# Decoder layer on one core: the first half-group of the self-attention in two blocks of 256 queries

## The reference

```python
q = x @ W_q
latent_kv = (k + v) @ W_down_kv
k_rec = (latent_kv @ W_up_k)...                 # 16 heads of 8 dimensions
v_rec = (latent_kv @ W_up_v)...
scores = einsum('bhqd,bhkd->bhqk', qh, k_rec) / sqrt(d)
decay = exp(-0.01 * abs(t[:, None] - t[None, :]))
attn = softmax(scores * decay, axis=-1)         # all 1024 keys for each of 1024 queries
out = einsum('bhqk,bhkd->bhqd', attn, v_rec) ... @ W_o
# then: logits = (x' @ W.T + b) @ ctx.T + mask, softmax, @ ctx; then the feed-forward net
```

## Time and profile before

| | |
|---|---|
| time, median of 3 runs | 554.35 us (554.33 to 556.05) |
| the profiled execution | 554.33 us, span 552.6 us |
| TensorE busy | 499.6 us (90%) |
| VectorE busy | 362.4 us (66%) |
| ACT busy | 336.2 us (61%) |
| GpSimd busy | 171.1 us (31%) |
| chain that ended last | PE 72%, DVE 20%, issue 3%, DMA 2%, ACT 2% |
| mean granted TensorE clock | 0.963 of 2.4 GHz |

### The profile page before, as it was taken

One profiled execution on the slowest core, in us unless ns is written; L12 is line 12 of the kernel. 1 busy time (PEld: TensorE's weight loads), 2 busy tenths in 40 slices (PEclk: granted clock), 3 DMA queues, 4 the chain that ended last, 5 costly groups with the idle time before them and its releaser, 6 DMA issues.

```text
span 552.6 us, 9809 instructions
## 1 busy us (share of the span) xinstructions
PE 499.6 (90%) x3494; PEld 327.1 (59%) x3494; DVE 362.4 (66%) x874; ACT 336.2 (61%) x659; POOL 171.1 (31%) x292
## 2 busy tenths in 40 slices
PE   8359999999999999989979979989797997989997
PEld 7206333333333333324549979879797997878886
DVE  6889988888788878704454466646666465654344
ACT  4627778787778777876664826537373562737420
POOL 6810125444444453235442221321222122210000
PEclk9758999999999999999999989989999998999999
DMA  8985400051007000031696423333342333300000
GB/s 243 284 256 121 88 2 2 4 134 41 1 3 166 10 2 2 1 117 39 165 325 187 124 76 116 93 114 92 83 121 79 116 91 115 114 16 6 1 6 7
DMA packets 27957, 49.23 MB, mean 89 GB/s; under 512 B 4140, under 2 KB 15860, under 8 KB 27332
## 3 DMA queue, kind: packets, MB, share of 16 engines
q1 hardware_dynamic: 27156, 47.87, 31.3%
q0 software_dynamic: 224, 0.54, 0.4%
q10 hardware_dynamic: 528, 0.18, 0.2%
HBM read 43.67 MB, written 4.72 MB: 88 GB/s over the span
## 4 chain that ended last, share of the span: by engine, by line
PE 72%; DVE 20%; issue 3%; DMA 2%; ACT 2%; POOL 1%; SPq 0%; DVEq 0%; ACTq 0%; POOLq 0%
PE banks L975 48%; PE banks L1084 11%; PE banks L1240 6%; DVE banks L802 6%; PE banks L1095 2%; DVE logits L878 2%; DVE fa L914 1%; PE banks L980 1%; DMA operands<-query_parts 1%; DVE qc_lo L849 1%; DVE xn L923 1%; DVE fa L913 1%; DVE fa L909 1%; ACT probs L669 1%; DVE f_small L905 1%
## 5 line engine op out<-in xcount | busy, mean ns | idle before, releaser
L669 ACT ACTIVATE probs<-banks 128x512 f32<-128x512 f32 x288 | 160.2, 599 | 49.1 <-PE banks L975 43.5
L802 DVE CUSTOM_DVE_ANT_0 banks<-banks,decay 128x1024 f32<-128x1024 f32 x128 | 155.0, 1244 | 31.4 <-PE banks L975 30.8
L975 PE MATMUL banks<-operands 112*128 112x512 bf16 (+4 forms) x736 | 148.0, 332 | 21.2 <-DMA operands<-query_parts 14.2
L975 PEld LDWEIGHTS banks<-operands 115*128 115x128 bf16 (+1 forms) x736 | 55.2, 98 | 126.9 <-ACT probs L669 55.1
L975 PEld LDWEIGHTS banks<-mem,pT 128*128 128x128 f32 (+1 forms) x816 | 108.5, 196 | 7.9
L975 PE MATMUL banks<-mem,pT 128*128 128x128 f32 (+1 forms) x816 | 112.1, 280 | 0.0
L690 ACT ACTIVATE pT<-banks 128x512 f32<-128x512 f32 (+1 forms) x104 | 60.4, 581 | 53.7 <-PE banks L1240 53.7
L878 DVE CUSTOM_DVE_ANT_0 logits<-banks,mring 128x512 f32<-128x512 f32 (+1 forms) x85 | 56.2, 667 | 43.2 <-PE banks L975 22.0
L532 POOL TENSOR_SCALAR_AFFINE_SELECT probs<-probs 128x128 f32<-128x128 f32 x128 | 37.3, 294 | 108.8 <-ACT probs L669 106.9
L1084 PE MATMUL banks<-probs,v_ext 128*32 128x512 f32 x512 | 68.2, 605 | 0.1
L975 PE MATMUL banks<-memT_hi,qc_hi 128*128 128x512 f32 (+1 forms) x104 | 51.0, 491 | 18.7 <-DVE cmax L878 18.7
(11 more groups left out here) (170 smaller groups left out, 515.4 us busy)
## 6 DMA issues: line engine op xcount, KB each, us to landing
mring<-in_mask_BxSxS_ik SPq DMA_DIRECT2D x39, 512.0 KB, 3.5
operands<-key_parts SPq DMA_DIRECT2D x24, 192.0 KB
operands<-query_parts SPq DMA_DIRECT2D x21, 192.0 KB
key_parts<-operand_parts SPq DMA_DIRECT2D x10, 256.0 KB, 3.3
mem<-in_ctx SPq DMA_DIRECT2D x3, 832.0 KB, 8.9
mask<-in_mask_BxSxS_ik SPq DMA_DIRECT2D x9, 256.0 KB, 2.9
pT<-in_mask_BxSxS_ik SPq DMA_DIRECT2D x9, 256.0 KB, 3.0
query_parts<-operand_parts SPq DMA_DIRECT2D x4, 384.0 KB, 5.3
```

The source lines that it names most:

```text
L669: act.activation(probs[:, to, :], PS[:, u % 3, :], ACT.Exp).then_inc(s_p, 1)
L802: dve.tensor_tensor_reduce(out=rows, in0=rows, in1=decay[:, off:off + S], scale=1.0, scalar=-3.0e38, op0=ALU.mult, op1=ALU.max, accum_out= ...
L975: return pe.matmul(o, a, b, start=start, stop=stop, skip_group_check=alone)
```

## The change

The first half-group is done in two blocks of 256 queries. Its units go tile by tile instead of head by head, so that after 8 units the maxima of the first 256 queries are there for all four heads. `BOUNDS` is 8, 16, 32, 48, ... 128; there are nine sets of shift rows. Set 0 (8 rows) goes out with six DMAs of SP and six of ACT, set 1 with twelve of SP, the others with six as before. Pairs 0 and 1 are the first block, pairs 2 and 3 the second: a score unit is then one key tile for two heads. The loop starts after 15 turns (`FIRST_TURNS`), and pairs 0 to 7 have five turns each, so that from pair 8 on the turns stand as before (15 + 40 = 23 + 32).

`parts_sb` moves into the second operand buffer, which frees ACT's first copy of the memory from its wait; instead GpSimd waits for the written parts before it sets that buffer's spare rows. TensorE turns three chunks of memory ahead of the first unit and one chunk in each of the next ten turns. SP's order becomes: group 0 in, `load_shift(0)`, group 1's lower operands, `load_shift(1)`, group 1's upper operands, `load_shift(2)`, `load_shift(3)`. The weight scales move to units 46, 64 and 80, the quantization to pairs 7 to 27.

```diff
+    FIRST_TURNS = 15
+    FULL_LEAD_PAIR = 8
+    HALF_PAIRS = 4
+    HQ = BANK // 2
+    BOUNDS = [UNITS // 2] + [UNITS * (g + 1) for g in range(NG * NH)]
+    MEM_FIRST = 3
     MEM_FRONT = 19
-    SCALE_UNITS = (28, 36, 44)
-    QUANT_PAIR = 3
-    MEM_UNIT = 8
+    SCALE_UNITS = (46, 64, 80)
+    QUANT_PAIR = 7
...
-            parts_sb = sb0("operand_parts", [P, 4, PARTS, S], BF16)
...
+        parts_sb = ops[1][:, :, :, :].rearrange("p w h n -> p (w h n)")[:, 0:4 * PARTS * S].rearrange(
+            "p (w i n) -> p w i n", w=4, i=PARTS)
...
+        def turns_of(n):
+            if n < FULL_LEAD_PAIR:
+                return FIRST_TURNS + 5 * n, 5
+            return UNITS + MAX_LEAD + 4 * n, 4
...
+        def half_keys(n):
+            qb = n // 2
+            off = [kt for kt in range(NT) if kt // 2 != qb][n % 2 * 3:n % 2 * 3 + 3]
+            return [off[0], 2 * qb + n % 2] + off[1:]
...
+        def load_half_shift(eng, i, w):
+            for part in range(PARTS):
+                for t in range(2):
+                    q0 = i * HQ + t * P
+                    eng.dma_start(queries(0, w, 0)[SHIFT_ROW + part:SHIFT_ROW + part + 1, :, q0:q0 + P],
+                                  shift_parts[t * HG:(t + 1) * HG, part, :]).then_inc(s_sh[i], 16)
...
-            def load_shift(hg):
+            def load_shift(i):
+                hg = max(i - 1, 0)
                 g, half = hg // NH, hg % NH
-                sp.wait_ge(s_sp, hg + 1)
+                sp.wait_ge(s_sp, i + 1)
                 for w in (QL, QU):
...
+                    if i == 0 and w == QL:
+                        load_half_shift(sp, 0, QL)
+                    if i == 1:
+                        load_half_shift(sp, 1, w)
...
             load_operand(0, QU)
             load_operand(0, KU)
+            load_shift(0)
             load_operand(1, KL)
             load_operand(1, QL)
-            load_shift(0)
+            load_shift(1)
             load_operand(1, QU)
             load_operand(1, KU)
-            load_shift(1)
             load_shift(2)
+            load_shift(3)
...
             pool.wait_ge(s_iota2, 1)
+            pool.wait_ge(s_scr0, 16)
+            for w in range(4):
+                pool.wait_ge(s_scr[w], 16 * (SLOTS if w in (KL, KU) else 1 if w == QL else NH))
...
-                if c == 0:
-                    act.wait_ge(s_scr0, 16)
...
                 if step >= MEM_LAG:
                     mem_low(step - MEM_LAG)
+            act.wait_ge(s_sp, 1)
+            load_half_shift(act, 0, QU)
...
+                if i >= 1:
+                    dve.wait_ge(s_sh[(i - 1) % 2], shift_count(i - 1))
+                link(dve.tensor_scalar(part[:, 0, :], src, -1.0, None, ALU.mult))
+                dve.scalar_tensor_tensor(rest, src, -1.0, part[:, 0, :], ALU.mult, ALU.subtract)
+                link(dve.scalar_tensor_tensor(part[:, 1, :], src, -1.0, part[:, 0, :], ALU.mult, ALU.subtract))
+                dve.tensor_tensor(part[:, 2, :], rest, part[:, 1, :], ALU.subtract).then_inc(s_sp, 1)
...
-                    pe.wait_ge(s_sh[hg % 2], 16 * 2 * PARTS * (hg // 2 + 1))
+                    i = hg + 1 if hg else 0
+                    pe.wait_ge(s_sh[i % 2], shift_count(i))
+                if n == 2 and j == 0:
+                    pe.wait_ge(s_sh[1], shift_count(1))
...
+                elif n < HALF_PAIRS:
+                    kt, q0 = half_keys(n)[j // 2], n // 2 * HQ
+                    for i in range(2):
+                        h = j % 2 * 2 + i
+                        for m, (kq, c0, c1) in enumerate(half_side(n, kt)):
...
+                if gb // 2 < HALF_PAIRS:
+                    pe.wait_ge(s_sel, gb // 2 * 5 + 4)
+                    qb = gb // 4
+                    for m in range(gb % 2 * 2, gb % 2 * 2 + 2):
+                        kt = half_keys(gb // 2)[m]
+                        for h in range(HG):
+                            last = pe.matmul(PS[h * VW:(h + 1) * VW, 3, qb * HQ:(qb + 1) * HQ], v_ext[:, kt, g * HG + h, :],
+                                             probs[:, 2 * m + h // 2, h % 2 * HQ:(h % 2 + 1) * HQ],
...
-            for mu in range(UNITS + MAX_LEAD):
+            pe.wait_ge(s_scaled, NH * 4)
+            for step in range(MEM_FIRST):
+                mem_tiles(step)
+            for mu in range(FIRST_TURNS):
                 max_turn(mu)
-                step = mu - MEM_UNIT
-                if 0 <= step < NC:
-                    mem_tiles(step)
-                if MEM_LAG <= step < NC + MEM_LAG:
-                    mem_rest(step - MEM_LAG)
+                if mu < NC:
+                    mem_rest(mu)
+                if mu + MEM_FIRST < NC:
+                    mem_tiles(mu + MEM_FIRST)
             pe.wait_ge(s_mlo, NC)
             for n in range(PAIRS):
-                mu = UNITS + MAX_LEAD + 4 * n
+                mu, turns = turns_of(n)
...
                 scores(n, 5)
                 early(n, 5)
+                if turns == 5:
+                    max_turn(mu + 3)
                 scores(n, 6)
...
-                max_turn(mu + 3)
+                max_turn(mu + turns - 1)
```

More of the change, by code:

```diff
@@ L273, in unit, with bounds_below, behind_bound, rows_slot @@
             return head, (half if on else 1 - half) * TPB + pair, half
[L277 to L281 removed]
+        def bounds_below(mu):
+            return sum(b < mu for b in BOUNDS)
+        def behind_bound(mu):
+            at = [i for i, b in enumerate(BOUNDS) if b <= mu]
+            return (at[-1], mu - BOUNDS[at[-1]]) if at else (None, UNITS)
+        def max_slot(mu):
+            return (mu + bounds_below(mu)) % 2
+        def rows_slot(i):
+            return (BOUNDS[i] + 1 + i) % 2
+        def shift_count(i):
+            return 16 * 2 * PARTS * (i // 2 + 2)
+        def rows_of(i):
+            return slice(BOUNDS[i - 1] if i else 0, BOUNDS[i])
+        def max_of(mu):
+            if mu < UNITS:
+                return 0, mu % HG, mu // HG
+            return mu // UNITS, mu % UNITS // TPB, mu % TPB
+        def turns_of(n):
+            if n < FULL_LEAD_PAIR:
+                return FIRST_TURNS + 5 * n, 5
+            return UNITS + MAX_LEAD + 4 * n, 4
+        assert sum(turns_of(FULL_LEAD_PAIR - 1)) == turns_of(FULL_LEAD_PAIR)[0]
+        def half_keys(n):
+            qb = n // 2
+            off = [kt for kt in range(NT) if kt // 2 != qb][n % 2 * 3:n % 2 * 3 + 3]
+            return [off[0], 2 * qb + n % 2] + off[1:]
+        def half_side(n, kt):
+            qb = n // 2
+            if kt <= 2 * qb:
+                return (("lower", 0, HQ),)
+            if kt > 2 * qb + 1:
+                return (("upper", 0, HQ),)
+            return (("lower", P, HQ), ("upper", 0, P))
         NMASK = (NT - 1) * NMP - EARLY_MASKS // 2
@@ L528, in _ @@
                 d0 = 2 * n % NT // 2 * P
-                for j in (0, 2, 4, 6):
-                    diag = probs[:, j, d0:d0 + P]
+                for i in range(4):
+                    if n < HALF_PAIRS:
+                        j = 2 + i // 2
+                        d = i % 2 * HQ + n % 2 * P
+                    else:
+                        j, d = 2 * i, d0
+                    diag = probs[:, j, d:d + P]
                     pool.wait_ge(s_p, n * PU + j + 1)
@@ L815, in weight_scales, with shift_split @@
                 dve.tensor_scalar(inv, inv, TIE_DOWN, None, ALU.mult).then_inc(s_fsc, 1)
[L817 to L825, removed]
+            def shift_split(i):
+                rows = rows_of(i).stop - rows_of(i).start
+                dve.wait_ge(s_mT, i + 1)
+                src = PS[0:rows, 4 + 2 * rows_slot(i), 0:P]
+                part, rest = shift_parts[0:rows, :, :], shift_r[0:rows, 0, :]
+                if i >= 1:
[4 more added lines that the diff above has]
+                dve.tensor_tensor(part[:, 2, :], rest, part[:, 1, :], ALU.subtract).then_inc(s_sp, 1)
             dve.wait_ge(s_tab, 3)
@@ L853, in max_turn @@
             def max_turn(mu):
-                if mu >= UNITS and mu % UNITS == 1 and mu < NG * NH * UNITS + UNITS:
-                    shift_split(mu // UNITS - 1)
+                bound, behind = behind_bound(mu)
+                if behind == 1:
+                    shift_split(bound)
                 if mu < NG * NH * UNITS:
@@ L1036, in max_unit, with max_rows @@
                 last.then_inc(s_mx, 1)
-            def max_rows(g):
-                pe.wait_ge(s_mxd, UNITS * (g + 1))
-                pe.transpose(PS[0:UNITS, 4 + 2 * rows_slot(g), 0:P], row_max[:, g * UNITS:(g + 1) * UNITS], ident[:, :]).then_inc(s_mT, 1)
+            def max_rows(i):
+                rows = rows_of(i)
+                pe.wait_ge(s_mxd, rows.stop)
+                pe.transpose(PS[0:rows.stop - rows.start, 4 + 2 * rows_slot(i), 0:P], row_max[:, rows], ident[:, :]).then_inc(s_mT, 1)
             def scores(n, j):
@@ L1064, in scores @@
                         last = side("diag", h, kt, slice(d0, d0 + P), start=(h == 0), alone=True)
+                elif n < HALF_PAIRS:
```

(16 more changed lines are left out.)

27 lines of the change are left out of this document (13 added, 14 removed).

## The result

| | before | changed |
|---|---|---|
| time, median | 555.56 us (5 runs, 554.33 to 556.05) | 566.73 us (5 runs, 565.62 to 567.31) |
| ratio | | 1.0208, 95% interval 1.0186 to 1.0231 |
| profiled execution | 554.33 us, span 552.6 | 567.11 us, span 565.3 |

What follows compares the result with a forecast made beforehand. VectorE's maxima bound the kernel before the loop over pairs, TensorE's own work inside it. Terms -6.6 + 3.5 + 0.8 + 4.6 + 1.1 + 3.0 = +6.4 us on 554.33 gave 560.7 us, range 555.5 to 565.5.

Steps and rivals of the forecast that it cites:

- start of the loop: Loop over pairs starts at 54.9 us instead of 61.51, once the first shift rows land: -6.6 us, bounds 4.5 to 8.
- maxima in the loop: Eight maxima move into pairs 0 to 7 and are paid in TensorE time, 0.44 us each: +3.5 us.
- half blocks: Pairs 0 to 3 do the same columns in more, shorter instructions: +0.8 us, bounds 0.1 and 1.7.
- stop before pair 4: TensorE stands still before pair 4 for the third set of shift rows: +4.6 us, bounds 4.0 and 6.0.
- clock behind the stops: Half clock after the pauses before the loop and before pair 4: +1.0 and +2.0 us, bounds 0 and 5 together.
- bunching on VectorE: Weight scales just ahead of the splits, with five maxima a pair, overload VectorE: +1.1 us, range 0.3 to 1.5.
- Rival (3): Loop starts no earlier, at 60 us or later, since ACT's copies or loads behind them end late: 564.8 us, chance 0.07.
- Rival (2): The wait for shift rows before pair 4 is covered: 554.1 us, or 553 if the first pause spares the clock; chance 0.12.
- The straight line through value products of unlike length: From 512- and 128-column times, estimated 256-column value products in pairs 0 to 3: at most +0.15 us per group of eight.
- Rival (5): In pairs 0 to 3, weight loads no longer hide behind half the columns: 3.8 us for 0.8, 563.7 us, chance 0.10.
- rival (1): The clock doesn't fall in the pauses before the loop and pair 4, or falls only inside them: 557.7 us, chance 0.17.
- rival (4): Transposes ahead of the loop leave the clock at half, so the loads land near 64 us: 569.8 us, chance 0.04.

Runs made afterwards that it cites:

- the late start: The changed kernel with its loop started after 23 turns, four turns in every pair: ratio 1.0152; with SP also waiting for the first shift rows, 1.0069 (pair 6.39 us).
- The experiment with SP's wait: The changed kernel, with SP loading the second buffer's operands only once all twelve loads of the first shift rows have landed: 561.83 us, ratio 1.0119.
- e2_six_turns: The changed kernel with six turns in each of pairs 0 to 3 and four from pair 4 on: 560.37 us, ratio 1.0109.
- e3_late_start: The changed kernel with the loop started after 23 turns and four turns in every pair, without SP's wait: 563.72 us, ratio 1.0152.
- e5_lead_19: The changed kernel with SP's wait, 19 turns ahead of the loop and five turns only in pairs 0 to 3: 554.18 us, ratio 0.9991.
- e4_kept_warm: The changed kernel with TensorE turning the identity 48 times while waiting before the loop and 32 times before pair 4: 561.69 us, ratio 1.0133.
- e6_lead_19_warm: As e5_lead_19, with four turns of the identity added behind each of turns 13 to 18: 553.49 us, ratio 0.9972 against the kernel before.
- e8_lead_19_scales: As e6_lead_19_warm, with the weight scales at units 40, 56 and 72: 553.44 us, ratio 0.9974 against the kernel before.

## Why the prediction was right or wrong

Up to pair 8 the sum said +6.4 us, and the mark moved by 10.8. Term by term:

| term | predicted | measured | from |
|---|---|---|---|
| start of the loop | -6.6 | -2.7 | 61.51 to 58.84 |
| maxima in the loop | +3.5 | +3.5 | a pair 6.82 us (74.94 to 81.76) for 6.37 |
| half blocks | +0.8 | 0 | the same 6.82, and 6.39 in the late start |
| stop before pair 4 | +4.6 | +5.0 | the idle time in its row |
| clock behind the stops | +3.0 | +3.8 | half of 3.53 and of 4.03 us |
| bunching on VectorE | +1.1 | +1.2 | what is left |
| sum | +6.4 | +10.8 | |

**The start of the loop is the step that failed**, by 3.9 of the 4.4 us, and the prediction had named it as a sign of being wrong ("if the loop starts after 58 us"). All of it up to the issue was right: the first maximum at 33.45, full clock from 35.1, turn 14 at 50.7, ACT's issues from 49.1 to 53.3 (I had the sixth starting at 51.9 to 52.7; it started at 52.7). The mis-sized term is the landing. I wrote 1.7 us, at most 3.0, and added a little because the second buffer's operands "now run at the same time"; it took 6.0. The experiment with SP's wait brings 3.6 us of it back, and the packets show the rows between those of the big loads. The bound of 3.0 came from rows that couldn't give it: it is the set issued at 183.2 us, when the DMA engines were at most 15% busy, and no set of the kernel before was sent with an operand load of 192 KB still under way (ahead of the first, at 55.5 us, the share had fallen to 0.00 at 53). The clue was there: in the kernel before, nine operand loads issued from 38.4 us to 42 kept the DMA engines busy until 52 us, 1.5 us each, so six of them are some 9 us of work (they took 7, from 51 to 58 us), and the last of the small loads was to be issued in the middle of it. **Rival (3)** is the nearest of the five: its loads behind ACT's copies did end late, but for the big loads beside them, which it didn't name, and it had the start at 60 or later.

**The stop before pair 4** was right in its place, its cause and within 0.4 us in its size. **Rival (2)** had the other sign on the condition that this stop is covered; with it covered (e2_six_turns) the kernel is still 1.1% slower, so the rival was too kind: the late landing, the half clock at the loop's start, the maxima moved into the loop and the 1.5 us of VectorE outweigh the early start. **Maxima in the loop** were exact. **Half blocks** were at my lower end: sixteen value products of 256 columns take the 1.00 us of eight of 512 (74.94 to 75.94). The straight line through value products of unlike length had put a constant on each instruction; these rows leave room for one for a whole run at most. **Rival (5)** is out by the same rows. **The clock** was inside its bounds (3.8 of 0 to 5); rival (1) is out. But the half clock at the loop's start isn't due to the stop alone: the clock fell at 52.1 us, 0.8 us after the last product of turn 14, and in e3_late_start and e5_lead_19, where the turns went on, it fell at 52.4 and 52.9 all the same. The kernel would have paid at the loop's start without the stop too. Here the Trainium skill's "TensorE: Matmul & The Clock Gate", Part 4, says that transposes do not count as busy for the clock, which led to my rival (4); e4_kept_warm, with the granted clock at 1.00 over 5.4 us of transposes alone, and the rise at 35.1 us are against it, so I was right to give it little. **Bunching** is a remainder in the table and was not measured by itself, but a part of it can be read. Between the loop's start and the mark TensorE's timeline has these waits for a maximum, first in the kernel before and then in the changed one, 1.0 us in all against 1.8, so 0.8 of the 1.2:

```profile
80.44 0.82 PE L975 MATMUL banks<-operands 112*128 112x512 bf16 x3 [0.51 <-DVE row_max L802]
106.70 0.82 PE L975 MATMUL banks<-operands 112*128 112x512 bf16 x3 [0.51 <-DVE row_max L802]
```

```profile
63.38 0.83 PE L1042 MATMUL banks<-operands 112*128 112x512 bf16 x4 [0.37 <-DVE row_max L866]
67.35 0.82 PE L1042 MATMUL banks<-operands 112*128 112x512 bf16 x4 [0.51 <-DVE row_max L866]
113.31 0.83 PE L1042 MATMUL banks<-operands 112*128 112x512 bf16 x4 [0.53 <-DVE row_max L866]
120.98 0.82 PE L1042 MATMUL banks<-operands 112*128 112x512 bf16 x4 [0.36 <-DVE row_max L866]
```

The one at 113.31 stands right behind the weight scales, which VectorE did from 110.75 us, in a pair of five turns. Where the pairs have four turns, the place of the scales makes no difference: e6_lead_19_warm and e8_lead_19_scales differ in nothing else, and take the same time from ACT's first issue to the mark. For units 64 and 80, which stand in pairs of four turns, I charged up to 0.7 us that nothing shows.

The other 0.4 us between mark and median, and the 2 us by which the profiled executions differ behind the mark, are of the size of one stretch at half clock behind the mark (six for five here); their number differs from one execution to the next.

What I didn't see at all is the second reader of the first landing. VectorE's second split waits for the first set of rows to have left its buffer. In the changed kernel VectorE stood idle then anyway; in the late start it cost 3.2 us. And the early turning of the memory took away the work that kept the clock up ahead of the loop: in the kernel before the memory's products filled the turns to the end.

## What to carry to other kernels

When a load of a few KB is on the path, look at everything that is issued within the time it takes to land, on every queue, and hold the big loads back until it is there: a wait on the issuing engine gave 3.6 us here, and nothing later in the kernel waited for the loads that it held back. When a loop is started earlier by taking lead from it, count the lead again at each later place that lived on it, in time and not in turns, and give the idle engine (here VectorE, 7 us) its work during the wait; with 19 turns ahead of the loop instead of 15 and SP's wait the same change goes from 2% slower to level, and with transposes in the thin turns to 0.3% faster. Compare single executions at a mark behind the change, not at their ends, and count from a mark ahead of it.

## What the runs showed of the hardware

Six loads of shift rows on ACT's queue landed 6.0 us after the last was issued while six loads of 192 KB ran from SP's queue, and 1.6 us after it (the last issue at 53.5, the rows there at 55.1) when they were held back. From 53 to 58 us 32 packets of ACT's queue ran between 214 of SP's, which took 73.9% of the 16 engines' time.

48 fp32 transposes back to back held the granted clock at 1.00 from 51.4 to 56.8 us (e4_kept_warm); in the changed kernel, with TensorE idle there, it stood at 0.50 from 52.2 us.

TensorE's granted clock fell to half at 52.4 us in e3_late_start and at 52.9 us in e5_lead_19 with no pause longer than 0.6 us before it, in turns of 1.18 us with two bf16 products of 512 columns in each; with four transposes more in each turn it stayed at full (e6_lead_19_warm, e8_lead_19_scales). At half clock such turns alone did not raise it, in the kernel before from 34.9 to 41.7 us.
